# State-space slots with the decay matrix folded to 768 columns

## What is computed

```
dA  = exp(A[h] * dt[t, h])
S_t = dA * S_(t-1) + B_t (outer) x_t
y_t = C_t . S_t + D[h] * x_t
```

## Time and profile before

| | us |
|---|---|
| runs | 3071.63, 3059.62, 3059.40 |
| median | 3059.62 |
| span of the profiled execution (first to last instruction) | 3067.1 |
| time of the profiled execution | 3071.63, the only one of the three that is not below the span; 4.5 lie around it |
| part before the slots | about 1500 |
| the slots | about 1500 to 3067 |

### The profile page before, as it was taken

The page is one execution under the profiler, slowest core; times in us unless marked ns, Lnnn a source line. Parts: engine busy times, 40 slices in busy tenths (PEclk is TensorE's granted clock), DMA queues, the critical chain, the costliest instruction groups (busy, mean ns, idle before and its releaser), DMA issues.

```text
span 3067.1 us, 58582 instructions
## 1 busy us (share of the span) xinstructions
PE 2711.5 (88%) x17318; PEld 2120.1 (69%) x17318; DVE 2384.6 (78%) x5972; ACT 2110.9 (69%) x4670; POOL 1973.4 (64%) x1697
## 2 busy tenths in 40 slices
PE   4799999998569888379799999999999999999997
PEld 2466666665469765267588788787887878878786
DVE  3466666666377589558599999998899999999896
ACT  4444454443255466346599999998999999999996
POOL 3322222214424214555399999998999999999998
PEclk7799999997889899689899999999999999999999
DMA  6355445455766544446777776767666666676673
GB/s 168 94 176 170 168 165 185 149 195 168 238 178 199 168 154 151 157 128 199 230 240 237 236 237 205 220 204 220 219 206 217 205 210 216 205 224 199 203 218 113
DMA packets 320436, 588.35 MB, mean 192 GB/s; under 512 B 47888, under 2 KB 138800, under 8 KB 319632
## 3 DMA queue, kind: packets, MB, share of 16 engines
q1 hardware_dynamic: 305776, 545.07, 57.6%
q0 software_dynamic: 14352, 39.54, 3.5%
HBM read 464.44 MB, written 124.17 MB: 192 GB/s over the span
## 4 chain that ended last, share of the span: by engine, by line
POOL 34%; issue 10%; ACT 3%; DVE 1%; PE 1%; DMA 1%; POOLq 1%; SPq 0%; ACTq 0%; DVEq 0%
POOL mm L2706 8%; POOL y L2719 7%; POOL yz L2723 7%; POOL y L2733 6%; POOL y_lo L2712 6%; ACT mt L2636 1%; DVE cv L2789 1%; DMA wi<-ssm_wi_split 1%; POOLq L2382 1%; ACT ys L2650 0%; ACT mt L2656 0%; DVE bank L2860 0%; ACT L2671 0%; POOL first L2748 0%; PE bank L64 0%
## 5 line engine op out<-in xcount | busy, mean ns | idle before, releaser
L2706 POOL TENSOR_TENSOR mm<-mt,cb 128x512 f32<-128x512 f32 x384 | 490.2, 1299 | 56.9 <-ACT mt L2656 54.9
L2636 ACT ACTIVATE mt<-a_wide,a_tok 128x128 f32<-128x128 f32 x1536 | 487.1, 389 | 3.5 <-POOL mm L2706 2.5
L2789 DVE SCALAR_TENSOR_TENSOR cv<-bank,taps,cv 128x509 f32<-128x509 f32 (+2 forms) x576 | 429.3, 745 | 13.6
L64 PE MATMUL bank<-f,wi 128*128 128x512 f32 x768 | 322.4, 420 | 14.7 <-DMA wi<-ssm_wi_split 14.6
L65 PE MATMUL bank<-f,wi 128*128 128x512 f32 x768 | 305.7, 398 | 0.0
L66 PE MATMUL bank<-f,wi 128*128 128x512 f32 x768 | 305.7, 398 | 0.0
L2723 POOL TENSOR_TENSOR yz<-y,zs 128x512 f32<-128x512 f32 x192 | 249.2, 1298 | 15.0
L2712 POOL TENSOR_TENSOR y_lo<-yz,y_hi 128x512 fp32r<-128x512 f32 x192 | 246.2, 1282 | 8.4 <-ACT y_hi L2661 6.5
L2719 POOL TENSOR_TENSOR y<-t 128x512 f32<-128x512 f32 x192 | 246.0, 1281 | 0.0
L2529 PE MATMUL bank<-mm,x_tok 128*64 128x128 f32 x3072 | 226.4, 283 | 13.1 <-POOL mm L2706 13.1
L2733 POOL TENSOR_TENSOR y<-y,ys 128x512 f32<-128x512 f32 x184 | 237.6, 1292 | 0.1
(11 more groups left out here) (476 smaller groups left out, 8067.5 us busy)
## 6 DMA issues: line engine op xcount, KB each, us to landing
wi<-ssm_wi_split SPq DMA_DIRECT2D x192, 512.0 KB
a_wide<-a_scratch SPq DMA_DIRECT2D x192, 512.0 KB
l_fw<-ffn_split SPq DMA_DIRECT2D x72, 768.0 KB
ea<-ea_scratch SPq DMA_DIRECT2D x384, 128.0 KB
wo<-ssm_wo_split SPq DMA_DIRECT2D x192, 256.0 KB, 4.1
sorted_scratch<-ex_zeros SPq DMA_DIRECT2D x96, 130.5 KB
ssm_wi_split<-l_s_out SPq DMA_DIRECT2D x24, 512.0 KB
ey_x<-sorted_scratch SPq DMA_DIRECT2D x94, 130.5 KB
```

What stands on the lines that cost most here:

```text
L64: pe.matmul(out, wh, xh, start=first, stop=False)
L2636: i = act.activation(mt[:, h, chunk(j)], a_wide[:, g % R, h, chunk(j)], ACT.Relu, bias=a_tok[:, s * NJ + j, 2 * t + h:2 * t + h + 1], scal ...
L2706: pl.tensor_tensor(mm[:, :, ts], mt[:, :, ts], cb[:, js, :].rearrange("p j t -> p (j t)") .unsqueeze(1).broadcast_to([P, 2, TS // 2]), ALU ...
L2789: dve.scalar_tensor_tensor(cv[:, a:TS], bank[:, X, 0:TS - a], taps[:, t, k:k + 1], cv[:, a:TS], ALU.mult, ALU.add).then_inc(ph["tap"], 1)
```

## The change

The 4 chunks j = 2u + q of a slot are regrouped: q counts two pairs, u the two chunks of a pair. On partitions 0 to 63 stand source tokens of chunk q, on 64 to 127 those of chunk q + 2. For each q the matrix has QW = 192 columns: 128 targets for the earlier 64 sources of the chunk, and 64 targets for the later 64 sources (their zero quarter is left out). That is 2 heads x 2 x 192 = 768 columns instead of 1024.

- `scores` becomes 16 matmuls on quarters of the array (64 x 64), 8 of 128 and 8 of 64 columns. Half of the source tokens stand on the wrong half of the partitions in `x_tok`; a new tile `x_swap` holds them.
- `swap_halves(k)`, the last step of SP's iteration k, waits for x_tok(k) and issues two DMAs from `x_tok` to `x_swap`, each 64 partitions of 1 KB (64 KB). `scores` waits for both.
- `a_wide` holds 256 instead of 512 columns per head, loaded by two DMAs (128 KB each) instead of one of 512 KB.
- `differences`: still 8 activations, 4 of 128 and 4 of 64 columns. `decays` and `decayed`: two operations of 384 instead of 512 columns each.
- update's results move to the upper halves of two PSUM banks; own_tokens reads the lower halves.
- `front` makes `cb` in the new layout: per stretch 8 matmuls with 64 stationary columns instead of 4, one more ScalarE copy (a_rows, 48 x 512), and once a mask of 192 columns.

```diff
                 def scores(g):
                     done(pe, "x_tok", g)
                     done(pe, "t2", g - 1)
-                    for j in range(NJ):
-                        if j % 2 == 0:
-                            done(pe, "mm", g * 2 + j // 2)
-                        for h in range(2):
-                            i = pe.matmul(bank[h * PH:(h + 1) * PH, INTRA, chunk(j)], x_tok[:, j, h * PH:(h + 1) * PH],
-                                          mm[:, h, chunk(j)], start=True, stop=True)
+                    done(pe, "x_swap", g, 32)
+                    for q in range(2):
+                        done(pe, "mm", g * 2 + q)
+                        first = (x_tok[ROWS[0], q, :], x_swap[ROWS[1], q, :])
+                        second = (x_swap[ROWS[0], q, :], x_tok[ROWS[1], q + 2, :])
                         for h in range(2):
+                            for u in range(2):
+                                hs = slice(h * PH, (h + 1) * PH)
+                                pe.matmul(bank[hs, LOCAL + u, q * P:(q + 1) * P], first[u][:, hs], mm[ROWS[u], h, q, 0:P],
+                                          start=True, stop=False, tile_position=(u * CH, h * PH))
+                        for h in range(2):
+                            for u in range(2):
+                                hs = slice(h * PH, (h + 1) * PH)
+                                i = pe.matmul(bank[hs, LOCAL + u, q * P + CH:(q + 1) * P], second[u][:, hs], mm[ROWS[u], h, q, P:QW],
+                                              start=False, stop=True, tile_position=(u * CH, h * PH))
...
+                def swap_halves(g):
+                    done(sp, "x_tok", g)
+                    sp.dma_start(x_swap[ROWS[1]], x_tok[ROWS[0], 2:4, :]).then_inc(ph["x_swap"], 16)
+                    sp.dma_start(x_swap[ROWS[0]], x_tok[ROWS[1], 0:2, :]).then_inc(ph["x_swap"], 16)
...
                     if k == (NS - 1) * NCT + 4:
                         start()
+                    if has(k):
+                        swap_halves(k)
...
-                    sp.dma_start(a_wide[:, g % R], a_drams[s // NS][2 * t:2 * t + 2, step(s)].partition_broadcast(P))\
-                        .then_inc(ph[f"wide{g % R}"], 16)
+                    for u in range(2):
+                        a = s % NS * TS + u * TS // 2
+                        sp.dma_start(a_wide[ROWS[u], g % R], a_drams[s // NS][2 * t:2 * t + 2, a:a + TS // 2].partition_broadcast(CH))\
+                            .then_inc(ph[f"wide{g % R}"], 16)
...
-                    for j in range(NJ):
-                        i = act.activation(mt[:, h, chunk(j)], a_wide[:, g % R, h, chunk(j)], ACT.Relu,
-                                           bias=a_tok[:, s * NJ + j, 2 * t + h:2 * t + h + 1], scale=-1.0)
+                    for q in range(2):
+                        for r, a, b, o in ((0, 0, P, 0), (1, P, QW, CH)):
+                            i = act.activation(mt[:, h, q, a:b], a_wide[:, g % R, h, q * P + o:(q + 1) * P], ACT.Relu,
+                                               bias=a_tok[:, s * NJ + 2 * q + r, 2 * t + h:2 * t + h + 1], scale=-1.0)
...
-                        pl.tensor_tensor(mm[:, :, ts], mt[:, :, ts], cb[:, js, :].rearrange("p j t -> p (j t)")
-                                         .unsqueeze(1).broadcast_to([P, 2, TS // 2]), ALU.mult).then_inc(ph["mm"], 1)
+                        pl.tensor_tensor(mm[:, :, q], mt[:, :, q], cb[:, s, q].unsqueeze(1).broadcast_to([P, 2, QW]), ALU.mult)\
+                            .then_inc(ph["mm"], 1)
```

More of the change, by code:

```diff
@@ L45 @@
 OUT_ROWS = FIRST_ROW + 2 * B * T
+QW = P + CH
 _cols = {}
@@ L1576, in front @@
         b_feat = sb("b_feat", [P, TS])
-        q = sb("dt_q", [HM, 12, TS])
-        absz, ez, u, lnu, d, corr, ru, mx, dt, adt, a_log, rest = (q[:, i, :] for i in range(12))
+        q = sb("dt_q", [HM, 13, TS])
+        absz, ez, u, lnu, d, corr, ru, mx, dt, adt, a_log, rest, a_rows = (q[:, i, :] for i in range(13))
         ends = sb("dt_ends", [HM, NJ])
@@ L1729, in scores @@
                     done(pe, "c_feat", c)
-                    for j in range(NJ):
-                        o = c * TS + j * P
-                        i = pe.matmul(bank[:, 4, j * P:(j + 1) * P], b_feat[:, j * P:(j + 1) * P],
-                                      st["c_feat"][:, o:o + P], start=True, stop=True)
+                    for q in range(2):
+                        for u in range(2):
+                            rows, o, w = slice(u * CH, (u + 1) * CH), q * QW, (2 * u + q) * P
+                            seen = st["c_feat"][:, c * TS + w:c * TS + w + P]
+                            pe.matmul(bank[rows, 4, o:o + P], b_feat[:, w:w + CH], seen, start=True, stop=True)
+                            i = pe.matmul(bank[rows, 4, o + P:o + QW], b_feat[:, w + CH:w + P], seen[:, CH:], start=True, stop=True)
                     i.then_inc(ph["cb_ps"], 1)
@@ L1737, in tokens @@
                     done(pe, "wend", c)
+                    done(pe, "a_rows", c)
                     done(pe, "lg", min(c + 1, G - 1))
-                    for m, src in ((0, a_log), (1, rest)):
+                    for m, src in ((0, a_rows), (1, rest)):
                         for j in range(NJ):
@@ L1836, in _ @@
                         act.activation(ru, a_log, ACT.Exp).then_inc(ph["ea"], 1)
+                        done(act, "at_ps", c - 1)
+                        act.activation(a_rows.rearrange("p (m u t) -> p m u t", m=NJ, u=2),
+                                       a_log.rearrange("p (u m t) -> p m u t", m=NJ, u=2), ACT.Copy).then_inc(ph["a_rows"], 1)
                         done(act, "rest", c)
@@ L2348, in ssm @@
         wo = sb("wo", [P, R, 2 * MP_OUT], F32R)
-        a_wide = sb("a_wide", [P, R, 2, TS])
+        a_wide = sb("a_wide", [P, R, 2, TS // 2])
         ea = sb("ea", [P, R, TS])
@@ L2361, in ssm @@
         x_tok, xd = sb("x_tok", [P, NJ, P]), sb("xd", [P, NJ, P])
-        mt, mm = sb("mt", [P, 2, TS]), sb("mm", [P, 2, TS])
+        mt, mm = sb("mt", [P, 2, 2, QW]), sb("mm", [P, 2, 2, QW])
+        x_swap = sb("x_swap", [P, 2, P])
         t1, t2 = sb("t1", [P, TS]), sb("t2", [P, 2, TS])
@@ L2369, in ssm @@
         acc = sb("acc", [P, KD, TS])
-        X, Z, XT, INTRA, INTER, UPD, OUT = 1, 0, 2, 3, 4, 5, 6
+        X, Z, XT, LOCAL, INTER, OUT = 1, 0, 2, 3, 5, 6
+        ROWS = (slice(0, CH), slice(CH, P))
         K0, NU = 6, NS * NJ
@@ L2395, in chunk, with upd @@
             return slice(j * P, (j + 1) * P)
+        def upd(j):
+            a = TS // 2 + j % 2 * P
+            return bank[:, LOCAL + j // 2, a:a + P]
         def before(g, j):
@@ L2654, in decays @@
                     for q in range(2):
-                        ts = slice(q * TS // 2, (q + 1) * TS // 2)
-                        act.activation(mt[:, :, ts], mt[:, :, ts], ACT.Exp, scale=-1.0).then_inc(ph["ex"], 1)
+                        act.activation(mt[:, :, q], mt[:, :, q], ACT.Exp, scale=-1.0).then_inc(ph["ex"], 1)
                 def output_high(g):
@@ L2837, in own_tokens, with halves @@
                     done(dve, "y", g - 2)
-                    dve.scalar_tensor_tensor(t2[:, g % 2], xs[:, g % 2], vec[:, g % NCT, 5:6], bank[:, INTRA, :],
-                                             ALU.mult, ALU.add).then_inc(ph["t2"], 1)
+                    def halves(a):
+                        return a.rearrange("p (u t) -> p u t", u=2)
+                    dve.scalar_tensor_tensor(halves(t2[:, g % 2]), halves(xs[:, g % 2]), vec[:, g % NCT, 5:6],
+                                             bank[:, LOCAL:LOCAL + 2, 0:TS // 2], ALU.mult, ALU.add).then_inc(ph["t2"], 1)
                 def state_part(g):
```

21 lines of the change are left out of this document (13 added, 8 removed).

## The result

The changed kernel takes 3986.05 us (median of four runs, 3975.24 to 4011.19); the kernel before took 3060.15 beside it. The ratio is 1.304 [1.299, 1.309]: slower by 926 us, where 730 were forecast. The profiled execution is the slowest of the four, 4011.19 us with a span of 4009.4; rows of before are compared with that one.

A forecast was written before the change was run, and what follows sets the result against it. The prediction took POOL as the bound, PE close behind, then the swap's loop: 11.1 us plus 0.6 for the clock, 11.7 instead of 7.91 per beat. Over 192 beats +728 us: 3800 profiled, 3790 median, range 3500 to 4080.

The forecast's parts named there:

- The mechanism: On SP, the swap behind ea and wo, which wait for t1, makes a loop of 11.1 us per beat; chance 0.80.
- x_tok alone: Rival: SP's own issues are not in the loop, only x_tok is; 9.4 us per beat, 3346 us; chance 0.10.
- The hidden swap: Rival: the swap lands without delaying scores, POOL sets the beat at 7.35 us, 2953 us; chance 0.03.
- high end: Range's upper limit: every beat cold, middling landing, 13.0 us, and a little of the longer landing, 13.3; 4080 us.
- DVE 3.24: Loop term on DVE: from the start of scan to the end of t1, 3.24 us.
- SP 1.80: Loop term on SP: picking up t1, then issuing ea and wo ahead of the swap, 1.80 us.
- landing 3.7: Loop term: the swap's two issues and its landing, 3.7 us, with ends of 3.15 and 4.25.
- scores 1.1: Loop term on PE: scores as 32 records on quarters of the array, 1.1 us.
- the quarters do run together: On PE, in scores; the rival had them not running together: scores 2.3 us, 4230 us; chance 0.07.
- a third of 1.9: PE's clock loss after the gap: 1.9 us per cold beat, taken for a third of the time, 0.6 us.
- the sum's 11.7: Forecast beat: the loop's 11.1 us plus 0.6 us for the clock, instead of 7.91 us.
- 192 times the same beat: Step to the total: 192 x (11.7 - 7.91) = +728 us on the profiled 3071.6, giving 3800 us.

The follow-up runs named there:

- No swap: The changed kernel without the two swap DMAs and PE's wait for them, scores reading unswapped rows of x_tok: 3018.1 us.
- swap first: The changed kernel with the swap's two issues ahead of since_start and weights_out in SP's iteration: 3275.34 us.
- four ea buffers: The changed kernel with four ea buffers instead of three, so ea's load waits for an older t1; swap still last on SP: 3288.85 us.
- PE kept busy: The changed kernel with ten added matmuls of 128 columns that nobody reads, ahead of scores' wait for the swap: 3862.38 us.
- both together: The changed kernel with scores and own_tokens one beat later, and the swap first in SP's iteration: 3037.0 us, 0.992 of the kernel before.

## Why the prediction was right, and where its size came from

**The mechanism held**, step by step. The swap is issued behind ea and wo, which wait for t1; t1 and x_tok come within 0.7 us of each other; PE waits 3.7 us per slot. No swap, swap first and four ea buffers each cut the loop at another place, and each took the time the way the loop says; the latter two took out twice the 1.8 us of SP's work, since landing and clock went with it. Of the rivals, x_tok alone (9.4 us) is what swap first makes of the kernel, at 8.22, because the landing is 2.83 there and not 3.7. The hidden swap, the rival on the other side, could have been worth 39 us at most, not 107: its step "POOL then sets the beat at 7.35, PE being just able to follow" fails by the prediction's own rows, in which PE has 7.77 - 1.15 + 1.1 = 7.72 us of work; measured, PE and DVE hold the typical beat at 7.46. The prediction's high end has a slip too: 13.3 us make 3060 + 192 x 5.39 = 4095, not 4080. The result lies inside either.

**The terms.** DVE 3.24 against 3.26 measured; SP 1.80 against 1.81; landing 3.7 against a median of 4.01; scores 1.1 against 0.92 in the turn shown and 0.83 warm (4.80 - 3.97 in the kernel with PE kept busy), so the quarters do run together. The Trainium skill (TensorEngine Tiling (Array Packing), Key Properties) has a drain of TensorE at a change of tiling mode. Between the last quarter and update no gap is to be seen in the turn shown: the quarter's row runs from 2808.79 to 2809.10, and update's starts at 2809.03.

**The clock** was in the sum with a third of 1.9 us, 0.6 per beat. Kept busy, PE's ordinary beats are 10.86 us on the average instead of 11.90: the clock cost 1.0 or a little more, since even there update is slow in 45 of 191 slots. The third came from two windows of another stage, the second of which the prediction calls free of such a gap. It has one, of 2.72 us, and the matmuls behind it are the slow ones of that window:

```profile
1312.64 0.42 PE L2180 MATMUL bank<-tab,ey_h 128*96 128x128 f32 x1 [2.72 <-issue]
```

So no row showed how often the clock would fall in this loop. Update does: from its start to from_state's it takes over 1.6 us in 143 of 191 slots, where the kernel before has a median of 0.99. The clock is low there in three quarters of the beats, and each pays less than 1.9. It fell at another place than I had it, too: in the turn shown scores is nearly warm and update pays, where I had the first matmuls after the gap paying most. That the sum's 11.7 lies within 0.2 of the ordinary beat is partly luck: a clock and a landing taken too short stand against scores taken too long.

**What was missing** is the larger part. The profiled run is 211 us above the sum's 3800. Of 191 beats, 146 are ordinary, with 11.90 us on the average where I had 11.7: 146 x 0.20 = 29 us. The first 32 after the start average 14.83: 32 x 3.13 = 100 us. 13 more lie above 15 us, 236.6 us together: 236.6 - 13 x 11.7 = 85 us. Both groups come from one step of the prediction, 192 times the same beat. The first has this on PE and DVE:

```profile
1703.05 2.07 PE L2575 MATMUL bank<-xd,b_tok 128*128 128x128 f32 x8
...
1706.46 0.38 PE L2592 MATMUL bank<-tab 128*128 128x128 f32 x2
1706.94 0.42 DVE L2845 TENSOR_TENSOR tab<-bank,tab 128x256 f32<-128x256 f32 x1 [6.54 <-PE bank L2592]
1707.28 0.46 DVE L2868 SCALAR_TENSOR_TENSOR part<-chain,dec,bank 128x64 f32<-128x64 f32 x2
```

Update ends at 1705.12, and scan starts at 1707.28: row_added stands ahead of it on DVE and waits for two matmuls that PE does after from_state. In the kernel before, the same 32 slots took 7.86 us in the median and the others 7.69, so it cost little there; in the loop it is 2.2 us per beat. Moving it took away 83 of the 100. Of the long beats the rare steps on SP make most:

```profile
2892.01 0.58 SPq L2458 DMA_DIRECT2D wo<-ssm_wo_split  x1
2892.64 0.60 SPq L2493 DMA_DIRECT2D out_dram<-acc  x1
2896.92 0.57 SPq L2489 DMA_DIRECT2D acc<-acc_scratch  x1
2897.53 0.61 SPq L2453 DMA_DIRECT2D x_swap<-x_tok  x1
```

The swap, last in the iteration, is issued 4.9 us later, behind a store of `acc` (2892.64) and its reload. With the swap ahead of them the excess of the long beats over 11.7 falls from 85 to 95.3 - 6 x 11.7 = 25 us. The 6 that remain were not tried.

So the time lay in the range, in its upper half, and the sum was low because it took the ordinary beat for all of them, not because of the clock alone.

## What to carry to other kernels

Before a transfer goes into a chain that had none, follow the issuing engine's program backwards from it: each wait and each issue ahead of it becomes part of the loop, the rare ones too. A small transfer whose place is fixed belongs first in its queue, or a whole stage ahead of its use; both together made the only full version of the split that gained here. And when a bound is relieved by 7%, look at the second and third engine before counting the gain: here DVE and PE left 3% of the typical beat.

## What the runs showed of the hardware

The landing of the same two transfers of 64 KB from SBUF to SBUF had a median of 2.83 us with the swap first on SP, 4.01 right behind 512 KB in SP's queue, and 4.69, up to 8.73, from ScalarE's queue beside SP's loads. What had just been issued counted, not the queue: in the last of these runs the median was 2.90 in the 32 slots without a load of SP in the 3 us ahead, and 5.90 in the 45 slots behind 512 KB or more.

Matmuls that nobody reads made the kernel 3% faster (3862.38 against 3986.05), with a granted clock of 0.92 instead of 0.83.
